# Fetching expert rows three experts ahead and adding filler products in a one-core Trainium2 kernel

## The reference

```python
x = x + L0_xattn(layernorm(x), ctx)            # attention on ctx, 16 heads of 8
x = x + L0_ffn(layernorm(x))                   # shared expert + 7 routed ones
x = x + L1_xattn(layernorm(x), ctx, ...)       # two attentions, an LSTM of 64 steps, then an MLP
x = x + L1_ffn(layernorm(x))                   # 8 experts, one per token, capacity 320

# L1_ffn: gates = softmax(tokens @ wg); expert = argmax(gates)
# pos = the token's rank among those that chose the same expert; kept if pos < 320
# y[token] = gate * (relu(token @ w1[e] + b1[e]) @ w2[e] + b2[e]), 0 where not kept
```

## Time and profile before

| | us |
|---|---|
| median of 3 runs | 735.28 |
| lowest and highest | 735.28, 737.05 |
| the profiled execution, its own time | 732.37 |
| its span | 730.5 |
| granted TensorE clock, mean over the span | 0.961 of full |

### The profile page before, as it was taken

One profiled execution on the slowest core, in us unless ns is written; L12 is line 12 of the kernel. 1 busy time (PEld: TensorE's weight loads), 2 busy tenths in 40 slices (PEclk: granted clock), 3 DMA queues, 4 the chain that ended last, 5 costly groups with the idle time before them and its releaser, 6 DMA issues.

```text
span 730.5 us, 16700 instructions
## 1 busy us (share of the span) xinstructions
PE 671.1 (92%) x6573; PEld 575.7 (79%) x6579; DVE 449.8 (62%) x1177; ACT 337.1 (46%) x914; POOL 120.8 (17%) x221
## 2 busy tenths in 40 slices
PE   6699999999999999989999998999999999777595
PEld 2487778988988889967777676999999999574574
DVE  5499857748756656689999998333343444531343
ACT  1589852333222222357888786455554544101121
POOL 2225730040000000034000010000000000037434
PEclk9899999999999999999999999999999999858699
DMA  8500200000000000033322100000000010402100
GB/s 256 180 20 17 62 2 1 1 1 1 1 1 1 1 1 0 9 96 85 92 67 68 36 7 2 1 2 1 15 9 23 1 26 13 93 20 84 30 20 22
DMA packets 30088, 25.03 MB, mean 34 GB/s; under 512 B 3887, under 2 KB 26801, under 8 KB 29762
## 3 DMA queue, kind: packets, MB, share of 16 engines
q1 hardware_dynamic: 28418, 20.91, 10.2%
q0 software_dynamic: 1600, 3.15, 1.4%
HBM read 19.33 MB, written 5.51 MB: 34 GB/s over the span
## 4 chain that ended last, share of the span: by engine, by line
PE 79%; DVE 9%; issue 3%; SPq 3%; another core or an unknown queue 2%; ACT 1%; DMA 1%; POOLq 0%; POOL 0%; DVEq 0%
PE SC L692 16%; PE PT L702 12%; PE MI L619 5%; PE SC L879 5%; PE PT L609 5%; PE SC L600 3%; PE SC L797 3%; PE SC L839 2%; PE SC L968 2%; PE SC L844 2%; PE SC L803 2%; PE PJ L582 2%; PE SC L800 2%; PE PT L850 2%
## 5 line engine op out<-in xcount | busy, mean ns | idle before, releaser
L1097 ACT ACTIVATE big<-SC 128x512 f32<-128x512 f32 x88 | 52.6, 600 | 144.5 <-PE SC L692 144.4
L702 PEld LDWEIGHTS PT<-wd,big 128*128 128x128 f32 (+1 forms) x768 | 90.2, 191 | 2.8 <-issue 0.4
L702 PE MATMUL PT<-wd,big 128*128 128x128 f32 (+1 forms) x768 | 90.7, 274 | 0.0
L1424 DVE TENSOR_TENSOR big<-SC,big 128x512 f32<-128x512 f32 (+1 forms) x88 | 60.6, 689 | 41.7 <-PE SC L692 32.4
L692 PE MATMUL SC<-xP,wgP 128*128 128x512 f32 x264 | 78.8, 407 | 0.7 <-DVE big L1424 0.3
L692 PE MATMUL SC<-xP,wuP 128*128 128x512 f32 x264 | 74.6, 391 | 0.0
L692 PEld LDWEIGHTS SC<-xP,wuP 128*128 128x128 f32 x264 | 49.5, 188 | 10.9
L619 PEld LDWEIGHTS MI<-vblk,PTs 128*64 128x64 f32 x1536 | 49.3, 138 | 10.9 <-ACT oT L1044 2.8
L619 PE MATMUL MI<-vblk,PTs 128*64 128x18 f32 x1536 | 53.8, 213 | 3.9 <-ACT big L1049 1.7
L1039 ACT ACTIVATE PTs<-PT 128x512 f32<-128x512 f32 x96 | 52.2, 595 | 7.1 <-PE PT L609 6.1
L609 PE MATMUL PT<-ident,sc 128*128 128x128 f32 x384 | 54.0, 285 | 0.6 <-ACT sc L1034 0.6
(11 more groups left out here) (257 smaller groups left out, 1293.5 us busy)
## 6 DMA issues: line engine op xcount, KB each, us to landing
kvs<-in_ctxT SPq DMA_DIRECT2D x32, 64.0 KB, 1.9
w1s<-in_e1w SPq DMA_DIRECT2D x8, 256.0 KB, 2.9
w2s<-in_e1w SPq DMA_DIRECT2D x8, 256.0 KB, 3.1
wg<-in_wg SPq DMA_DIRECT2D x1, 1408.0 KB, 9.1
wu<-in_wu SPq DMA_DIRECT2D x1, 1408.0 KB, 12.0
wd<-in_wd SPq DMA_DIRECT2D x2, 512.0 KB, 14.1
x_mid<-X SPq DMA_DIRECT2D x1, 1024.0 KB, 5.1
X<-x_mid SPq DMA_DIRECT2D x4, 256.0 KB, 4.8
```

The source lines that it names most:

```text
L702: last = pe.matmul(PT[:, e % 2, t * P:t * P + P], h[0:w, t * P:t * P + P], wd[0:w, e, c, :], start=(c == 0), stop=(c == 2))
L1097: act.activation(sg[a % 2], SC[:, a % 2, :], ACT.Silu).then_inc(s["silu_done"], 1)
L1424: last = dve.tensor_tensor(hT[e % 2][0:w, c, :], SC[0:w, 2 + a % 2, :], sg[a % 2][0:w, :], ALU.mult)
```

## The change

Three edits.

1. POOL issues the gathers of experts 0, 1 and 2 (8 of 20), waits for `out_stored`, and then for each expert e issues the gathers of expert e+3 and after them the scatters of expert e. Before, all 20 gathers came ahead of all scatters. Number and content of the DMAs are the same.
2. POOL's `gate_at` now waits for all four `lane_ready` counts, so it no longer runs beside DVE's `at_lane`.
3. Filler products on PE: 12 become 25 ahead of `rows_t` of the last group; 5 become 9 after its logits; 2 new ones before the wait for `sums_copied`; 13 new ones before the wait for `token_ready`; 10 become 12 (`BURST`) after the sum for `gate`.

```diff
-BURST = 10
+BURST = 12
+AHEAD = 3
@@ gpsimd
             pool.tensor_tensor(token_at, ...).then_inc(s["token_ready"], 1)
+            pool.wait_ge(s["lane_ready"], NT // 4)
             pool.tensor_tensor(gate_at, ...).then_inc(s["gate_ready"], 1)
             pool.wait_ge(s["rows_stored"], 2 * 64 * len(GROUPS))
             pool.wait_ge(s["home_ready"], 1)
-            for q in range(NQ):
-                pool.indirect_dma_start(xin[q], None, rows_in, ...home[:, q:q + 1]...
-                                        ).then_inc(xin_loaded[q * P // CAP], 16)
-            pool.wait_ge(s["out_stored"], 64)
-            for e in range(E1):
+            def gathers(e):
+                for q, r, _, _ in parts_of(e):
+                    if r == 0:
+                        pool.indirect_dma_start(xin[q], None, rows_in, ...home[:, q:q + 1]...
+                                                ).then_inc(xin_loaded[e], 16)
+            def scatters(e):
                 for j, (q, _, _, w) in enumerate(parts_of(e)):
                     if e % 2 == 1 or w == P:
                         pool.wait_ge(s["y_ready"], 3 * e + j + 1)
                         pool.indirect_dma_start(out, ...home[:, q:q + 1]..., xin[q][:, D:2 * D], ...)
+            for e in range(AHEAD):
+                gathers(e)
+            pool.wait_ge(s["out_stored"], 64)
+            for e in range(E1):
+                if e + AHEAD < E1:
+                    gathers(e + AHEAD)
+                scatters(e)
@@ tensor
-            keep_warm(SC[:, 1, :], 12)
+            keep_warm(SC[:, 1, :], 25)
             rows_t(3, 11, NT)
             pe.wait_ge(s["last_evacuated"], 1)
             rows_logits(3, 11, NT, SC[:, 0, :])
-            keep_warm(SC[:, 1, :], 5)
+            keep_warm(SC[:, 1, :], 9)
...
                       ).then_inc(s["sums_done"], 1)
+            keep_warm(SC[:, 1, :], 2)
             pe.wait_ge(s["sums_copied"], 1)
...
+            keep_warm(SC[:, 1, :], 13)
             pe.wait_ge(s["token_ready"], 1)
```

More of the change, by code:

```diff
@@ L523, in _ @@
             pool.wait_ge(s["home_ready"], 1)
-            for q in range(NQ):
-                pool.indirect_dma_start(xin[q], None, rows_in,
-                                        bass.IndirectOffsetOnAxis(ap=home[:, q:q + 1], axis=0),
-                                        bounds_check=T - 1, oob_is_err=False).then_inc(xin_loaded[q * P // CAP], 16)
-            pool.wait_ge(s["out_stored"], 64)
-            for e in range(E1):
+            def gathers(e):
+                for q, r, _, _ in parts_of(e):
+                    if r == 0:
+                        pool.indirect_dma_start(xin[q], None, rows_in,
+                                                bass.IndirectOffsetOnAxis(ap=home[:, q:q + 1], axis=0),
+                                                bounds_check=T - 1, oob_is_err=False).then_inc(xin_loaded[e], 16)
+            def scatters(e):
                 for j, (q, _, _, w) in enumerate(parts_of(e)):
```

## The result

| us | before | changed |
|---|---|---|
| median | 735.51 (735.28 to 737.05, 4 runs) | 726.86 (726.52 to 729.0, 4 runs) |
| the profiled execution, its span | 732.37, 730.5 | 726.52, 724.7 |

The ratio is 0.9888 (95% interval 0.9865 to 0.9911): 8.6 us faster, where 20 against the median, 18.7 in the working, had been forecast. The direction held. The gain is less than half of the forecast one, and the time lies inside the stated range only at its far end, 0.6 us short of it.

The account below looks back on a forecast made before the run. It took PE's sums at half clock and an unexplained wait during POOL's gathers as the bound; 13.7 + 5.0 = 18.7 us off 732.4 gave 713.7, or 716.6 against the median. Forecast 715, range 709 to 727.5.

Parts of the forecast that it names:

- the gap: PE idle 11.7 us after `expert_in(2)`, waits released by "remote" during POOL's 20 unbroken gathers; forecast to vanish.
- The term of 13.7 us: Gain from gathering three experts ahead: 11.6 us of waiting plus 2.1 us of lost clock in `expert_out(1)`.
- shorter gaps: Rival: signals held for some 3 to 5 issues, once or twice; 5 to 10 us come back, 722; shared chance 0.20.
- stretched issues: Rival: DVE work in four experts lengthens POOL's issues by 6.9 us, 2.7 covered; 719; shared chance 0.20.
- The refill of instruction memory: Possible cause at an engine, a late refill by DMA, under the rival of an unchanged wait: 730, chance 0.12.
- The head start: `expert_in(0)` starts sooner through filler and higher clock: about 4.4 us, up to 7.9; 5.0 taken.
- the short stretch: PE's time without wide products, 630.7 to 634.0, cut from 6.2 to 3.3 us; called not safe for the clock.
- the nine products: Filler after the last group's logits: if the clock falls, 3.8 us instead of 2.1, delaying the routing by 1.5 us.
- The sum for `home`: PE's first long sum, taken at full clock: about 4.1 us instead of 6.99, 2.9 gained.
- the sum for `gate`: PE's second long sum, taken to stay at half clock, so no gain of its own.
- The deadlines: Later gathers, queued among scatters on POOL, land before PE needs them; the nearest, `expert_in(7)`, has 2.7 us to spare.
- draining at changes of direction: Rival: POOL waits up to 3.6 us at each of eight gather-scatter changes; 722 to 743, chance 0.05.

Follow-up runs that it names:

- e8_filler: Changed kernel with all 20 gathers ahead of all scatters again, filler products and later gate_at kept; 731.98 us, ratio 0.9938, on an occasion with gaps.
- e5_after: Changed kernel unaltered, run again beside the kernel before on an occasion with gaps; 727.35 us, ratio 0.9876.
- e9_no_scatter: Changed kernel without the scatters of experts 0 to 6, on an occasion with gaps; 716.99 us, ratio 0.9758.
- e10_plain_rows: Changed kernel with the gathers of experts 3 to 7 as plain DMAs of other rows on SP, with gaps; 717.15 us, ratio 0.9751.
- e17_pauses: Changed kernel with POOL's order broken up by waits for landed gathers and finished scatters, on an occasion with gaps; 722.93 us, ratio 0.9821.
- e18_old_order_pauses: Changed kernel with all 20 gathers first again, but pauses among gathers and scatters, on an occasion with gaps; 720.75 us, ratio 0.9794.
- e11_no_data: Changed kernel with all 20 gathers first, those of experts 3 to 7 bounded to move next to no rows; 729.84 us, ratio 0.9929.
- e2_done: Not a run: the signal from PE that DVE waits on, given three times per expert in the kernel before and the changed one.
- e12_few_signals: Changed kernel with all 20 gathers first and PE signalling DVE once per expert instead of three times; 731.94 us, ratio 0.9953.
- e7_clock: Changed kernel with filler spread through the last routing stretch and both sums, 2 products instead of 12 after them; 729.80 us, ratio 0.9902.
- e14_pauses_clock: Changed kernel with pauses on POOL plus 3 more filler products after the last rows_t, on an occasion without gaps; 722.41 us, ratio 0.9979.
- e3_no_scatter: Changed kernel without the scatters of experts 0 to 6, on an occasion without gaps; 719.26 us, ratio 0.9943.
- e13_pauses: Changed kernel with POOL's order broken up by waits for landed gathers and finished scatters, on an occasion without gaps; 722.10 us, ratio 0.9985.

## Why the prediction was wrong

**The step that failed** is the one that took the gap as gone: "after it POOL's queue can't run on while DVE is held". That is not enough. A scatter stops POOL only if its rows are not ready yet. The five issues that go with an expert on average take 6.5 us, more than its 5.9, so POOL had fallen behind by expert 1, found its rows ready, and stopped only after ten issues. The working had this sum before it (20 issues from 665.1, 26.4 us without a break) and read it only as a deadline for the rows. The term of 13.7 us measured 4.2 in the profiled executions, and 4.6 at the medians (`e8_filler` against `e5_after`). The rival "shorter gaps" named the mechanism, but took up to five issues in a row where there were ten, a gap once or twice where there were three, and shared a chance of 0.20 with the stretched issues; 9.5 of the 13.7 us came back, inside its 5 to 10.

**What the gap is.** Runs show that it needs a long unbroken run of indirect DMAs on POOL (`e9_no_scatter`, `e10_plain_rows`, `e17_pauses`, `e18_old_order_pauses`), that the bytes moved don't matter (`e11_no_data`), nor the number of `e2_done` signals (`e12_few_signals`), and that it comes on some occasions only. The pauses put in are waits for the DMAs under way to land, so a stop of the issuing and an empty queue are not told apart. By which path POOL's issuing holds PE's signals, and why some occasions are free of it, stays open. The refill of instruction memory, the rival cited from the Trainium skill ("Runtime: NRT & Kernel Launch", section "Instruction fetch mechanics"), does not fit: between 648 and 692 us the trace of before has packets of q0 alone, though the gap ended at 681.3, and so has that of `e8_filler` between 650 and 688, though its waits ended at 678.2, 682.3 and 684.4. In the changed kernel one instruction packet, at 678.4, does coincide with the end of a wait, ACT's of 2.3 us, and with the end of none of the others.

**The head start** was a term of the right kind and the wrong size: 2.6 us in the trace and 3.7 at the medians (`e8_filler`), against 5.0, which was itself more than the 4.4 that its steps add up to. By these steps: the 25 products cost nothing, as said. The clock fell in the short stretch, which the text had called not safe and then left out of the sum. So the nine products delayed the routing, and that part gained 0.2 us instead of 1.5 (1.1 lost up to L952, 1.3 won after it). The sum for `home` took 3.95 us, 3.0 saved against 2.9 forecast; the sum for `gate` ran at half clock, as forecast; the twelve products took 3.84, not 3.2. In the traces of `e7_clock` and `e14_pauses_clock` the clock held through the routing and fell inside the sum for `home` instead. In the profiled execution of `e3_no_scatter` it held through the routing and the sum for `home`, and fell at about 646.5, in the sum for `gate`; that run took 713.2, the fastest of ten with a median of 719.3. Over these ten the time goes with the mean granted clock, from 713.20 us at 0.981 to 720.65 at 0.966, so when the clock falls is worth several us from run to run, and one trace can't price it.

**What was right.** Edit 2: at_lane took one operation of 1.24 us and three of 0.68, 3.3 against 3.2 forecast, and neither sum waited for gate_at. The deadlines: PE never waited for rows. No draining at changes of direction: 669.72 and 671.01 are a scatter and the gather after it, 1.29 us apart. No stretched issues: they stay at 0.98 to 1.06 us beside DVE's work, so what the Trainium skill ("SBUF — State Buffer", section "SBUF: two separate sides") says of DVE locking GpSimd out of the shared ports cost next to nothing here.

## What to carry to other kernels

When a gap has no cause in the trace but coincides with one engine's unbroken activity, don't book it as gone because the activity is reordered: work out how long the unbroken stretches are afterwards, and sum the gap over each. Issues at 1.3 us apiece can hold up other engines even where their own time is hidden, so it can pay to break them up with pauses; but put the pauses where POOL does not set the end, for in `e13_pauses` its last scatter came 4.7 us later, and on an occasion without gaps that took back 4.1 of the 5.3 us gained. Time an edit on more than one occasion when the thing it cures is not in the program: here its value was 4.6 us on one occasion and nothing on another.

## What the runs showed of the hardware

Indirect DMAs of 128 rows were issued about 1.3 us apart (1.28 to 1.45, the second of a kernel 1.57 after the first), whether they moved 131 KB or nearly nothing, read or wrote. In long runs of them PE's signals to DVE and ACT came late on four of six occasions, in the kernel before by 12.6 us (PE done at 668.7, DVE on at 681.29), and on the other two no trace shows it, in spite of runs of 22 and 27. How many it takes varied: in the first run of a kernel the signals were still on time after ten (at 665.5 before, at 663.9 after the change), in a later one a wait of 0.8 us followed six (`e17_pauses`). After runs of two to five the traces mark no wait as such. While the sums with 20 columns per product kept PE 100% busy, the clock did not rise (0.50 from 648.5 to 655.8), and in `e14_pauses_clock` it fell 1.7 us into them.
